# The edge sort of a graph recommender: a one-hot stored column by column, seven of eight column products on ScalarE, block targets from exact two-byte products

## The reference, cut to what matters

```python
h = emb; acc = emb                                  # N = 12501 rows of 128
for _ in range(2):
    h = segment_sum(adj_val[:, None] * h[adj_col], adj_row, num_segments=N)   # 150000 edges
    acc = acc + h
graph_item_embs = acc / 3
# then: gather 512 sessions of 50 items, attention over a session,
# scores = select @ l2norm(graph_item_embs).T       # 512 x 12501
```

## Time and profile before

| | |
|---|---|
| median of 3 runs | 4142.29 us |
| profiled execution, its own time | 4142.95 us |
| its span | 4141.2 us |
| first step of the sort (L876) starts | 73.86 us |
| last but one group evacuated (L642) | 664.78 us |
| end of the last scatter (L555) | 699.40 us |
| a group, groups 0 to 5 | about 31.6 us |
| a group, groups 6 to 17 | about 32.9 us |
| granted clock over the span | 0.757 |

### The profile page before, as it was taken

One profiled execution on the slowest core, in us unless ns is written; L12 is line 12 of the kernel. 1 busy time (PEld: TensorE's weight loads), 2 busy tenths in 40 slices (PEclk: granted clock), 3 DMA queues, 4 the chain that ended last, 5 costly groups with the idle time before them and its releaser, 6 DMA issues. The chain is left out here.

```text
span 4141.2 us, 69284 instructions
## 1 busy us (share of the span) xinstructions
PE 3114.1 (75%) x10054; PEld 1840.1 (44%) x10054; DVE 3033.3 (73%) x7214; ACT 877.0 (21%) x3009; POOL 2871.6 (69%) x2965
## 2 busy tenths in 40 slices
PE   6999995777777777777776777777777777776878
PEld 5777774333333333333333334333344433433444
DVE  8999995777777777777775776776767767776655
ACT  3999996000000000000001000000000000007443
POOL 1677766777777777777775777777777777775750
PEclk8899987777777777777776776776777777666889
DMA  1000000222222222222225222222222222247993
GB/s 36 4 3 3 3 3 23 56 55 55 55 55 55 55 55 55 55 55 55 55 54 161 56 55 55 55 55 55 55 55 55 55 55 55 55 115 98 70 114 157
DMA packets 162231, 235.38 MB, mean 57 GB/s; under 512 B 67554, under 2 KB 107776, under 8 KB 161952
## 3 DMA queue, kind: packets, MB, share of 16 engines
q0 software_dynamic: 92896, 171.14, 21.5%
q1 hardware_dynamic: 54132, 58.90, 4.4%
q10 hardware_dynamic: 15052, 3.83, 0.6%
HBM read 192.69 MB, written 41.01 MB: 56 GB/s over the span
## 5 line engine op out<-in xcount | busy, mean ns | idle before, releaser
L1456 PE MATMUL bank<-ring 128*128 128x256 f32 x4976 | 2168.1, 570 | 822.8 <-DVE ring L1117 795.3
L1456 PEld LDWEIGHTS bank<-ring 128*128 128x128 f32 x4976 | 1130.2, 264 | 1835.1 <-DVE ring L1117 1768.4
L1117 DVE TENSOR_SCALAR ring<-bank,mlo,mval 128x256 f32<-128x256 f32 x2488 | 1343.8, 540 | 710.5 <-DMA ring<-table,cring 356.8
L580 POOL DMA_INDIRECT ring<-table,cring x1195 | 1127.6, 944 | 397.0 <-issue 352.3
L580 POOL DMA_INDIRECT ring<-in_L_rec_emb,cring x1195 | 1131.7, 947 | 368.8 <-issue 355.6
L1166 DVE TENSOR_TENSOR acc<-acc,bank 128x256 f32 x2488 | 1019.2, 410 | 140.9 <-issue 140.0
L656 ACT ACTIVATE big<-big 128x68 f32<-128x68 bf16 x1764 | 557.4, 406 | 0.0
L1376 PE MATMUL bank<-big,ring 128*128 128x136 f32 x2352 | 438.8, 323 | 63.1 <-DVE ring L884 17.8
L549 POOL DMA_INDIRECT sorted_edges<-moved,block_to x313 | 397.2, 1269 | 101.3 <-issue 101.3
L1376 PEld LDWEIGHTS bank<-big,ring 128*128 128x128 f32 x2352 | 344.4, 210 | 151.6 <-ACT big L656 132.6
L672 ACT COPY mlo<-ring 128x24 f32 (+1 forms) x104 | 21.9, 211 | 1553.2 <-PE bank L1456 1519.3
(11 more groups left out here) (214 smaller groups left out, 1659.2 us busy)
## 6 DMA issues: line engine op xcount, KB each, us to landing
ring<-in_L_rec_emb SPq DMA_DIRECT2D x3136, 0.5 KB
ring<-in_L_rec_emb ACTq DMA_DIRECT2D x3136, 0.5 KB
ring<-table ACTq DMA_DIRECT2D x3136, 0.5 KB
ring<-table SPq DMA_DIRECT2D x3136, 0.5 KB
scores<-stage SPq DMA_DIRECT2D x48, 512.0 KB, 3.0
ring<-in_L_rec_emb,cring POOLq DMA_INDIRECT x1195, 3.7
ring<-table,cring POOLq DMA_INDIRECT x1195, 3.8
table<-big SPq DMA_DIRECT2D x7, 896.0 KB, 8.7
```

Source lines behind the costliest of these rows:

```text
L580: pool.indirect_dma_start(msg[:, s, :], None, source, bass.IndirectOffsetOnAxis(cring[:, s:s + 1], 0)).then_inc(s_g[s], 16)
L1117: dve.tensor_scalar(onehot[:, u % SR, :], bank[7][:, 0:BUCKET], mlo[:, u:u + 1], mval[:, u:u + 1], ALU.is_equal, ALU.mult).then_inc(s_S[u ...
L1456: pe.matmul(bank[u % PR][:, 0:BUCKET], msg[:, h * T + u, :], onehot[:, u % SR, :], start=True, stop=True).then_inc(s_mm[u % M], 1)
```

## The change

Three edits, all in the sort.

1. `hot_c` gets the layout `[step, column t, 68]`, so the 68 elements of a column are one run. `hot_columns` writes it in that order: the row of numbers is now its innermost axis and the place is repeated along it. Readers follow.
2. `CA` goes from 6 to 7: ScalarE issues 14 ACTIVATE instructions for a step instead of 12, VectorE's `last_columns` handles one column (136 elements) instead of two (272).
3. The block targets are computed with two-byte products. `below`, `steps`, `lscol`, `dscol`, `dsnow` have 114 rows: rows 0 to 49 as before, rows 64 to 113 a second copy that holds what the rounding of `dscol` to bf16 left over. `dscol`, `dsnow` are bf16, and the stationary operand is the upper half of each float32 one of `begun` (`begun_high`). `FAR` becomes 2^18. GpSimd has two memsets and two affine selects more in the setup, and VectorE one instruction more.

```diff
-    CA = 6
+    CA = 7
-        hot_c = carve(big, Q * LC * C // 2, BF16).rearrange("p (h c t) -> p h c t", h=Q, t=C)
+        hot_c = carve(big, Q * LC * C // 2, BF16).rearrange("p (h t c) -> p h t c", h=Q, t=C)
+        begun_high = begun.bitcast(BF16).rearrange("p (n w) -> p n w", w=2)[:, :, 1]
...
-                        last = act.activation(at_c[:, r, t, q, :], hot_c[:, r, :, t], ACT.Copy,
+                        last = act.activation(at_c[:, r, t, q, :], hot_c[:, r, t, :], ACT.Copy,
                                               scale=what[:, bass.ds(n * C + t, 1)])
...
-                dve.tensor_tensor(hot_c[:, r, :, :], row_c.unsqueeze(2).broadcast_to([P, LC, C]),
-                                  place_c[:, h, s * C:(s + 1) * C].unsqueeze(1).broadcast_to([P, LC, C]),
+                dve.tensor_tensor(hot_c[:, r, :, :], row_c.unsqueeze(1).broadcast_to([P, C, LC]),
+                                  place_c[:, h, s * C:(s + 1) * C].unsqueeze(2).broadcast_to([P, C, LC]),
                                   ALU.is_equal).then_inc(s_hc, 1)
...
                 dve.tensor_tensor(at_c[:, r, CA:C, :, :],
-                                  hot_c[:, r, :, CA:C].rearrange("p n t -> p t n").unsqueeze(2).broadcast_to([P, C - CA, 2, LC]),
+                                  hot_c[:, r, CA:C, :].unsqueeze(2).broadcast_to([P, C - CA, 2, LC]),
                                   pays[:, bass.ds(n * C + CA, C - CA), :].unsqueeze(3).broadcast_to([P, C - CA, 2, LC]),
...
-                dve.tensor_scalar(begun[0:NB + 1, 0:blocks * P], grid[0:NB + 1, :], lscol[:, bass.ds(g, 1)], None,
+                dve.tensor_scalar(begun[0:BOTH, 0:blocks * P], grid[0:BOTH, :], lscol[:, bass.ds(g, 1)], None,
...
-            dve.tensor_copy(dscol[:, :], bank[7][0:NB + 1, 0:GR]).then_inc(s_lcc, 1)
+            link(dve.tensor_copy(dscol[:, :], bank[7][0:BOTH, 0:GR]))
+            dve.tensor_tensor(dscol[UP:BOTH, :], bank[7][UP:BOTH, 0:GR], dscol[UP:BOTH, :], ALU.subtract).then_inc(s_lcc, 1)
...
-                    last = pe.matmul(bank[7][:, k:k + 1], begun[0:NB + 1, k * P:(k + 1) * P], dsnow[:, :],
+                    last = pe.matmul(bank[7][:, k:k + 1], begun_high[0:BOTH, k * P:(k + 1) * P], dsnow[:, :],
```

More of the change, by code:

```diff
@@ L78, in recommender_program @@
     NST = NT // T
-    FAR = float(2 ** 20)
+    FAR = float(2 ** 18)
+    UP = 64
+    BOTH = UP + NB + 1
     SR, PR, LEAD = 8, 4, 4
@@ L87, in recommender_program @@
     PER = NU // M
+    assert NT * P // R < FAR / R <= 2 ** 16 and NB + 1 <= UP
     assert T % M == 0 and NT - T < NU <= NT
@@ L214, in recommender_program @@
         gate = sb("gate", [P, 3])
-        below = sb("below", [P, NB + 1])
-        steps = sb("steps", [P, NB + 1])
+        below = sb("below", [P, BOTH])
+        steps = sb("steps", [P, BOTH])
         padded_i = sb("padded_i", [NB, GR], I32)
@@ L237, in recommender_program @@
         lstart = sb("lstart", [P, GR, NB])
-        lscol = sb("lscol", [NB + 1, GR])
-        dscol = sb("dscol", [NB + 1, GR])
-        dsnow = sb("dsnow", [NB + 1, 1])
+        lscol = sb("lscol", [BOTH, GR])
+        dscol = sb("dscol", [BOTH, GR], BF16)
+        dsnow = sb("dsnow", [BOTH, 1], BF16)
         block_id = sb("block_id", [P, NK])
@@ L532, in _ @@
             pool.memset(block_id[0:1, 0:SKIP], FAR).then_inc(s_cst, 1)
[L533 to L536, removed]
+            pool.memset(below[:, NB + 1:UP], 0.0).then_inc(s_cst, 1)
+            pool.memset(steps[:, NB + 1:UP], 0.0).then_inc(s_cst, 1)
+            for a in (0, UP):
+                pool.affine_select(out=below[:, a:a + NB + 1], in_=ones[:, 0:NB + 1], compare_op=ALU.is_gt, fill=0.0, base=0,
+                                   pattern=[[1, NB + 1]], channel_multiplier=-1).then_inc(s_cst, 1)
+                pool.affine_select(out=steps[:, a:a + NB + 1], in_=ident[:, 0:NB + 1], compare_op=ALU.not_equal, fill=-1.0,
+                                   base=-1, pattern=[[1, NB + 1]], channel_multiplier=-1).then_inc(s_cst, 1)
             def opened(n, waits):
@@ L848, in _ @@
                     count_group(g + 2)
-            dve.wait_ge(s_cst, 16)
+            dve.wait_ge(s_cst, 20)
             dve.wait_ge(s_lc, 1)
@@ L864, in _ @@
             dve.wait_ge(s_lc, 2)
-            dve.tensor_copy(lscol[:, :], bank[4][0:NB + 1, 0:GR])
+            dve.tensor_copy(lscol[:, :], bank[4][0:BOTH, 0:GR])
             link(dve.tensor_tensor(earlier[:, :], earlier[:, :], bank[4][0:NB, 0:GR], ALU.subtract))
@@ L1389, in _ @@
             edges_before(0, kept[:, 0])
-            pe.wait_ge(s_cst, 16)
+            pe.wait_ge(s_cst, 20)
             pe.wait_ge(s_lcc, 1)
@@ L1396, in _ @@
                 if n == 0:
-                    pe.matmul(bank[4][0:NB + 1, 0:GR], below[0:NB, :], padded[:, :], start=True, stop=True).then_inc(s_lc, 1)
+                    pe.matmul(bank[4][0:BOTH, 0:GR], below[0:NB, :], padded[:, :], start=True, stop=True).then_inc(s_lc, 1)
             pe.wait_ge(s_lcc, 2)
@@ L1400, in _ @@
             pe.wait_ge(s_lcc, 3)
-            pe.matmul(bank[7][0:NB + 1, 0:GR], steps[0:NB + 1, :], shift[:, :], start=True, stop=True).then_inc(s_lc, 1)
+            pe.matmul(bank[7][0:BOTH, 0:GR], steps[0:NB + 1, :], shift[:, :], start=True, stop=True).then_inc(s_lc, 1)
             pe.wait_ge(s_az, 2)
```

## The result

The changed kernel takes 4101.45 us (median of 4, 4100.1 to 4105.39) against 4144.59 us (median of 4) for the kernel before: ratio 0.9898, 95% interval 0.988 to 0.9915. That is 42 to 43 us less, where 46.5 were forecast (4096 us, with a range from 4087 to 4122). The experiments ran on three chips, on which the kernel before takes 4135.34, 4137.24 and 4136.44 us. On the third the changed kernel was measured again: 4091.76 us, ratio 0.9892 (0.9875 to 0.9909), 44.7 us less.

A forecast was written before the change was run, and what follows sets the result against it. VectorE was taken to bound the sort: 142 steps x 0.33 = 46.9 us, plus 0.9, less 0.3 for setup and 1 for GpSimd, gives 46.5 us saved. Forecast 4096 us, range 4087 to 4122.

The forecast's parts named there:

- VectorE bounds the sort, ScalarE is next: In the sort, VectorE bounds; ScalarE is 0.9 us (early groups) to 2.1 us (later ones) a group behind.
- L899 at 304 ns, 0.33 us a step: VectorE's last_columns falls from 634 to 304 ns, on 136 contiguous elements instead of 272, saving 330 ns a step.
- The ACTIVATE at 340 ns, one every 0.242 us: ScalarE's ACTIVATE in the sort falls from 406 to 340 ns; one begins every 0.242 us instead of 0.307.
- Rival A: ScalarE keeps 0.307 us between ACTIVATEs and bounds the sort: 52 us slower, 4194 us; chance 0.08.
- The rule on 16-byte lines: For hot_c reads: its two-accesses half fits the rows; its free 8-bf16 stride, by the letter, would leave ScalarE at 0.307 us.
- The break-even spacing in early groups: Spacing between ScalarE's ACTIVATEs at the point of change between VectorE and ScalarE: 0.247 us in early groups, 0.26 in later.
- An early group at 28.9 us: VectorE's early group in the sort shrinks by 8 x 0.33 = 2.64 us, to 28.9 us.
- The loss of 1 us that I took: GpSimd's slack in the sort shrinks from 3.3 to about 0.5 us a group, costing 1 us; 0 to 5 open.
- Targets and TensorE: nothing: TensorE's two-byte block targets change nothing either way: their cost fits under the 9.9 us in which step 5 is not ready.
- The setup, +0.3 us: Before the sort, converting dscol takes one dependent instruction more, 0.16 us plus the wait: +0.3 us.
- The sum: Over the sort: 142 x 0.33 = 46.9, plus 0.9, less 0.3 setup, less 1 GpSimd: 46.5 us saved.
- near 653: Sign of being right: the sort's last scatter on GpSimd ends near 653 us instead of 699.4.

The follow-up runs named there:

- The experiment: Changed kernel with TensorE's 16 products for the next group's edges_before issued ahead of step 0 in groups 0 to 5: 4087.57 us, ratio to the kernel before 0.9883.

## Why the prediction was right, and where not

- *VectorE bounds the sort, ScalarE is next.* Right: with the layout alone the time fell by 27.3 us, which is VectorE's shorter instruction (27.8), with ScalarE waiting 109 us.
- *L899 at 304 ns, 0.33 us a step.* Right (298 ns, 0.336). Its row was the fit through L884 and L876 and the check by L1316.
- *The ACTIVATE at 340 ns, one every 0.242 us.* Right: (3.50 - 0.34) / 13 = 0.243. The row that carried it was L755, the same form on a contiguous source. Rival A was priced at 52 us slower; made real it was 50.6.
- *The rule on 16-byte lines.* The Trainium skill, page "SBUF — State Buffer", section "Door 1", wants at least two accesses to each 16-byte line, and gives 8 bf16 as a stride that is free. The first half is what the runs show for VectorE (387 ns at a step of 16 bytes, 297 at 8). The second, read by the letter, does not hold: a step of exactly 8 bf16 is the slow one. The break-even spacing in early groups, by my own sum, is 0.249 us and not 0.247; nothing hangs on it.
- *An early group at 28.9 us.* The step that failed: it took 29.5. I had left out that VectorE's wait for TensorE's counts (2.1 us in five groups before) hangs on ScalarE's step 0. VectorE came 0.66 us earlier in steps 0 and 1, ScalarE only 0.3 us a step; that accounts for about 0.4 us of the 0.6 that the wait grew a group, and the rest is not explained. It cost 3.0 us of the 46.5, which is most of the miss. The experiment removed it, and the groups fell to 28.4, because the 0.4 us of wait that my 28.9 carried on went too.
- *GpSimd.* Its slack of about 3.3 us became 2.3 in the first turns and about 0.4 later. The loss of 1 us that I took did not come: scatter 17 begins 0.34 us after `evacuate` starts (618.93 and 619.27), 0.33 before.
- *Targets and TensorE: nothing.* Right in the number (ratio 1.0), but the reason was too good. The 9.9 us are the time between the starts of `hot_columns` for steps 4 and 5, and in it TensorE still has step 4 to do. In one group of the kernel before, the target loads ran from 483.04 to 486.92 us, while the partition one-hots of step 5 were ready at 485.33: TensorE came to step 5 1.6 us late. What hid this was the ring of four steps, not an idle TensorE.
- *The setup, +0.3 us.* Not seen: the first step starts anywhere from 72.6 to 73.9 us in these profiles, whatever the kernel.
- *The sum.* From its first step the sort took 625.5 us before and 580.7 and 581.3 us in the two profiles of the changed kernel: 44.8 and 44.3 less. Groups 6 to 17 gave 31.5 us, where 12 x 2.64 = 31.7 were due, groups 0 to 5 gave 12.8 for 15.8. The end "near 653" was met at 653.49 with some luck: in that profile the first step came 1.1 us earlier than before (72.76 and 73.86). In the second profile the sort ended at 655.19.

## What to carry to other kernels

Where two engines are within a few per cent of each other, look for the change that speeds both before you move work between them: here the layout gave 27.3 us, the move 17.1 us on top of it, and the same move without the layout cost 50.6 us. Price a strided operand by the slope between two instructions of its own form; where a read pays 1.78 ns an element beside 1.03, as here, look at how many elements it takes from each 16 bytes. And when a step gets shorter, go through every wait that stood just inside its cover, on engines that are far from busy as well.

## What the runs showed of the hardware

- **Two elements in 16 bytes are enough.** For bf16 read from SBUF, VectorE: 387 ns for 136 elements at a step of 16 bytes, 297 at 8, 298 at 2. ScalarE, fourteen instructions of 68 elements: 4.38 to 4.41 us, 3.57 to 3.61, 3.49. The 8-byte step was run once. Not tried: other types and larger steps.
- **Small GpSimd instructions stretch beside VectorE's scan.** Sixteen one-element additions took 2.35 us with VectorE's sort work over, 8.08 and 7.22 beside its scan (3.65 us) and the three two-byte products after it. The longest single one lasted 3.51 us.
- **TensorE's granted clock rose with nothing gained.** Over the sort (from 78 us to the last groups) it was 0.90 before and 0.89 in the changed kernel without its two-byte targets, against 0.94 with the targets alone and 0.94 and 0.93 in the two profiles of the changed kernel. The changed kernel without its two-byte targets, an early group:

```profile
109.14:138.63 29.49, 29.49 (x171) 25.59 (x170) 28.22 (x47) 28.24 (x122) 20.63 (x19) 0.83 0.03 5
```

Beside it stands the window 108.51:138.13 above. With float32 targets TensorE had no idle time at all by the record (29.49 of 29.49 us) with part of the group at the lower of its two levels (1.2 GHz), and with two-byte ones it had the full clock (2.4 GHz) and 1.65 us idle; both groups lasted about the same. Not every group differs so much: in the second profile of the changed kernel the same group had 0.94. With the float32 targets the granted clock was 1.00 up to 123 us, 0.68 from 123 to 126 and 0.50 from 126 to 132; their 34 loads began at 122.95 us and took 6.31 us, right behind the products of step 4. The third edit thus bought room on TensorE, which this kernel does not use.
